# The norm in front of the router, by rows: tokens centred and scaled while they stand as rows, then transposed back

## What is computed

```python
def _layernorm(x, axis=-1, eps=1e-05):
    m = jnp.mean(x, axis=axis, keepdims=True)
    v = jnp.var(x, axis=axis, keepdims=True)
    return (x - m) / jnp.sqrt(v + eps)
...
    x = x + _L0_xattn_ref(_layernorm(x, axis=-1), ctx_1024, ctx_1024, ...)
    x = x + _L0_ffn_ref(_layernorm(x, axis=-1), ...)
    x = x + _L1_xattn_ref(_layernorm(x, axis=-1), ctx_1024, ctx_1024, ...)
    x = x + _L1_ffn_ref(_layernorm(x, axis=-1), ...)
```

## Time and profile before

| | us |
|---|---|
| median of 3 runs | 335.76 (335.49 to 336.69) |
| profiled execution | 337.2 |
| its span | 335.0 |
| TensorE busy | 315.0 (94%) |
| VectorE busy | 262.3 (78%) |
| ScalarE busy | 201.6 (60%) |
| GpSimd busy | 45.8 (14%) |

### The profile page before, as it was taken

The page is one execution under the profiler, slowest core; times in us unless marked ns, Lnnn a source line. Parts: engine busy times, 40 slices in busy tenths (PEclk is TensorE's granted clock), DMA queues, the critical chain, the costliest instruction groups (busy, mean ns, idle before and its releaser), DMA issues.

```text
span 335.0 us, 4438 instructions
## 1 busy us (share of the span) xinstructions
PE 315.0 (94%) x1498; PEld 224.1 (67%) x1506; DVE 262.3 (78%) x543; ACT 201.6 (60%) x325; POOL 45.8 (14%) x55
## 2 busy tenths in 40 slices
PE   7999899899999899969879999999999999998995
PEld 7655698556556667656657777777767777766763
DVE  2542674769578997979987989989987996999693
ACT  3514206464687856688878758758367546635733
POOL 0030012121111701164171121000001000000000
PEclk9899999999999999999979999999999999999999
DMA  7999960000000000180440651001001000000001
GB/s 261 427 422 317 297 257 1 0 3 0 0 0 2 1 2 0 63 190 1 132 120 1 179 104 33 0 2 32 0 0 34 0 0 31 3 0 31 2 0 63
DMA packets 13173, 25.21 MB, mean 75 GB/s; under 512 B 608, under 2 KB 9056, under 8 KB 11872
## 3 DMA queue, kind: packets, MB, share of 16 engines
q1 hardware_dynamic: 11712, 20.75, 17.5%
q0 software_dynamic: 1440, 4.19, 6.8%
HBM read 16.55 MB, written 1.05 MB: 53 GB/s over the span
## 4 chain that ended last, share of the span: by engine, by line
PE 80%; DVE 8%; ACT 6%; issue 3%; DMA 2%; POOL 0%; SPq 0%; DVEq 0%; ACTq 0%; POOLq 0%
PE ps L1389 76%; DMA ctxT<-in_ctxT 2%; PE ps L1495 1%; PE ps L1612 1%; ACT ring L560 1%; ACT L610 1%; ACT L575 1%; ACT L560 1%; DVE hm_even L1070 1%; PE ps L1516 1%; ACT hid L612 1%; ACT hB L552 1%; DVE ctxT L1281 1%; DVE kv L1278 1%; DVE ctxT L1280 1%
## 5 line engine op out<-in xcount | busy, mean ns | idle before, releaser
L1389 PE MATMUL ps<-hm_even,ew_hi 128*128 128x512 f32 (+1 forms) x152 | 49.6, 420 | 1.9 <-ACT xi L538 1.2
L1389 PE MATMUL ps<-hm_odd,ew_hi 128*128 128x512 f32 (+1 forms) x148 | 47.6, 422 | 0.0
L1389 PEld LDWEIGHTS ps<-hm_even,ew_hi 128*128 128x128 f32 (+1 forms) x152 | 26.3, 188 | 8.4 <-issue 2.4
L1389 PEld LDWEIGHTS ps<-hm_odd,ew_hi 128*128 128x128 f32 (+1 forms) x148 | 25.7, 189 | 5.5 <-issue 0.5
L612 ACT ACTIVATE hid<-ps,pB 128x512 f32<-128x512 f32 x32 | 21.8, 687 | 11.6 <-PE ps L1389 10.9
L477 POOL TENSOR_TENSOR zz<-zz,mhalf 128x4 f32<-128x4 f32 x12 | 14.8, 1237 | 91.2 <-DVE zz L943 91.2
L1389 PE MATMUL ps<-hm_even,ew_lo 128*128 128x512 f32 (+1 forms) x72 | 25.2, 392 | 0.0
L1389 PE MATMUL ps<-x_hi,w1x_hi 128*128 128x512 f32 x40 | 19.1, 478 | 5.8 <-ACT hid L612 3.7
L1389 PE MATMUL ps<-hm_odd,ew_lo 128*128 128x512 f32 (+1 forms) x64 | 22.3, 394 | 0.0
L1051 DVE SCALAR_TENSOR_TENSOR ring<-ring,pB,hid 128x1024 f32<-128x1024 bf16 x16 | 20.5, 1281 | 0.6
L1389 PE MATMUL ps<-zz,pB 128*128 128x512 f32 (+3 forms) x52 | 19.4, 502 | 0.5 <-DVE zz L1324 0.5
(11 more groups left out here) (325 smaller groups left out, 769.0 us busy)
## 6 DMA issues: line engine op xcount, KB each, us to landing
ring<-in_fc1b SPq DMA_DIRECT2D x4, 1024.0 KB, 17.3
ring<-in_fc2a SPq DMA_DIRECT2D x4, 1024.0 KB, 12.4
hm_odd<-hm_odd SPq DMA_DIRECT2D x4, 512.0 KB, 3.1
packC<-in_packC SPq DMA_DIRECT2D x1, 1152.0 KB, 9.1
pB<-in_packB SPq DMA_DIRECT2D x1, 1077.0 KB, 9.9
ctxT<-in_ctxT SPq DMA_DIRECT2D x2, 512.0 KB, 6.4
a<-in_fc1a SPq DMA_DIRECT2D x1, 1024.0 KB, 8.9
xtok<-in_xtok SPq DMA_DIRECT2D x1, 1024.0 KB, 12.8
```

The costliest lines, as they stand in the source:

```text
L1389: return pe.matmul(out, lhsT, rhs, start=start, stop=stop)
```

## The change

For the norm in front of the router, mean and factor are applied where the token is a row: `ln_rows` subtracts the mean and multiplies by the factor straight out of the token bank, four VectorE instructions per chunk, into `xi`. `state_back` transposes those four pieces back on TensorE, ScalarE's `state_evac` copies them to `xi`. `center`, the spread of this norm and its multiplication are gone; those of the feed-forward norm stay. Who waited for `zn` now waits for `cx`; the token bank is held until the rows are read. In the first pass of the experts ScalarE's evacuations of chunks 2 and 3 move behind some hidden tiles.

```diff
+        def back_bank(c):
+
+            return bank[5] if c == NCH - 1 else bank[6]
...
+            def ln_rows(c):
+
+                n = LN["rt", c]
+                dve.wait_ge(sem("lrs"), n + 1)
+                for j in range(BPC):
+                    row = slice(j * D, (j + 1) * D)
+                    dve.tensor_scalar(xi[:, ck(c)][:, row], tok_bank(n)[:, row], lmv[:, n % 2, j, 0:1],
+                                      lrs[:, n, j:j + 1], ALU.subtract, ALU.mult).then_inc(sem("rows"), 1)
...
+            def state_evac(c):
 
                 act.wait_ge(sem("cx_ps"), c + 1)
-                act.activation(xi[:, ck(c)], center_bank(c)[:, :], ACT.Copy).then_inc(sem("cx"), 1)
+                act.activation(xi[:, ck(c)], back_bank(c)[:, :], ACT.Copy).then_inc(sem("cx"), 1)
...
                 if t == 3:
                     state_split(0)
                     route(0, 1)
+                if q:
+                    ln_rows(t - 2)
                 if a:
                     att_norm(t - 1)
-                if q:
-                    ln_scale("rt", t - 2)
                 ffn_add(t)
...
             att_pt(3)
-            ln_scale("rt", 2)
+            ln_rows(2)
             kept(0, 2)
...
                     lower(s, 1)
-                    ln_scale("rt", 3)
+                    ln_rows(3)
                     lower(s, 0)
...
-                if n >= 2:
+                if n - 2 in NORMED and n < 3 * NCH - 1:
+                    pe.wait_ge(sem("rows"), BPC * (NORMED[n - 2] + 1))
+                elif n >= 2:
                     pe.wait_ge(sem("lst"), BPC * (n - 1))
...
+            def state_back(c):
+
+                pe.wait_ge(sem("rows"), BPC * (c + 1))
+                if c == 0:
+                    pe.wait_ge(sem("zn"), NCH)
+                elif c < NCH - 1:
+                    pe.wait_ge(sem("cx"), c)
+                else:
                     pe.wait_ge(sem("squash"), 2)
                 for j in range(BPC):
...
+                    row = slice(j * 128, (j + 1) * 128)
+                    last = pe.transpose(back_bank(c)[:, row], xi[:, ck(c)][:, row], ident)
+                last.then_inc(sem("cx_ps"), 1)
...
-                if q:
-                    center(t - 2)
                 ffn_down(t, (0, 1))
                 if q:
-                    ln_spread("rt", t - 2)
+                    state_back(t - 2)
                 ffn_down(t, (2,))
...
             ln_tok("rt", 2, "x3")
-            center(2)
             hidden(0, (2, HT))
...
                     pe.wait_ge(sem("lg"), 2)
-                    pe.wait_ge(sem("cx"), 3)
+                    pe.wait_ge(sem("x3"), 3)
...
                         probs_t(3)
-                        ln_spread("rt", 2)
+                        state_back(2)
...
                     def hidden_0():
-                        center(3)
                         hidden(1, (0,))
 
                     def hidden_2():
                         hidden(1, (2,))
-                        ln_spread("rt", 3)
+                        state_back(3)
```

More of the change, by code:

```diff
@@ L391, in build @@
             LN["rt", c] = len(LN)
-        def spread_at(which, c):
-            return c if which == "ffn" else NCH + c
+        NORMED = {n: c for (which, c), n in LN.items() if which == "rt"}
         @block.sync
@@ L700, in _ @@
             expand_evac(1, 7, 6)
-            hidden_gelus(1, (1,))
-            center_evac(3)
-            hidden_gelus(1, (0, 2, 3))
+            hidden_gelus(1, (1, 0, 2))
+            state_evac(3)
+            hidden_gelus(1, (3,))
             r1_gelu(3)
@@ L944, in ln_stats, with ln_scale @@
                     .then_inc(sem("lve"), 1)
[L946 to L956, removed]
+            def ln_scale(c):
+                dve.wait_ge(sem("spread_ps"), c + 1)
+                if c >= 2:
+                    dve.wait_ge(sem("fh_ps"), FT * (c - 1))
+                dve.tensor_tensor(zT[:, c % 2, :], xT[:, ck(c)], bank[6][:, :], ALU.mult).then_inc(sem("zn"), 1)
+            def ln_rows(c):
[5 more added lines that the diff above has]
+                                      lrs[:, n, j:j + 1], ALU.subtract, ALU.mult).then_inc(sem("rows"), 1)
             def att_scores(c):
@@ L1503, in busy, with ln_spread @@
                     mm(out, ew2_hi[:, 0:D], ew2_hi[:, 0:CH])
-            def ln_spread(which, c):
-                n, at = LN[which, c], spread_at(which, c)
-                if at == 0:
+            def ln_spread(c):
+                n = LN["ffn", c]
+                if c == 0:
                     pe.wait_ge(sem("w1"), 2)
                 else:
-                    pe.wait_ge(sem("zn"), at)
+                    pe.wait_ge(sem("zn"), c)
                 pe.wait_ge(sem("lrs"), n + 1)
-                if at == 2 * NCH - 1:
+                for j in range(BPC):
+                    last = pe.transpose(bank[6][:, j * 128:(j + 1) * 128],
+                                        lrs[:, n, j:j + 1].to_broadcast([128, 128]), ident)
+                last.then_inc(sem("spread_ps"), 1)
+            def state_back(c):
+                pe.wait_ge(sem("rows"), BPC * (c + 1))
+                if c == 0:
+                    pe.wait_ge(sem("zn"), NCH)
+                elif c < NCH - 1:
+                    pe.wait_ge(sem("cx"), c)
+                else:
                     pe.wait_ge(sem("squash"), 2)
                 for j in range(BPC):
-                    last = pe.transpose(spread_bank(which, c)[:, j * 128:(j + 1) * 128],
-                                        lrs[:, n, j:j + 1].to_broadcast([128, 128]), ident)
-                last.then_inc(sem("spread_ps"), 1)
[L1520 to L1525, removed]
+                    row = slice(j * 128, (j + 1) * 128)
+                    last = pe.transpose(back_bank(c)[:, row], xi[:, ck(c)][:, row], ident)
+                last.then_inc(sem("cx_ps"), 1)
             def ffn_up(c, tiles):
-                pe.wait_ge(sem("zn"), spread_at("ffn", c) + 1)
+                pe.wait_ge(sem("zn"), c + 1)
                 for f in tiles:
```

35 lines of the change are left out of this document (16 added, 19 removed).

## The result

The changed kernel takes 347.43 us (median of 4 executions, 346.14 to 350.0), the kernel before 335.62 beside it: a ratio of 1.0358, 95% interval 1.0326 to 1.0391. It is slower by 11.8 us, in the direction that was forecast; 343.2 was given, and 347.43 lies 0.4 us above the range. The profiled execution is the one of 350.0 us, so its times are 2.6 us above the median.

The account below looks back on a forecast made before the run. TensorE was taken as the bound, other engines counting where it waits for them. Terms of -0.6, +1.45, +2.35 and +1.8 make +5.0; with +2.4 for the clock, 335.76 + 7.4 = 343.2 us, range 339.0 to 347.0.

Parts of the forecast that it names:

- TensorE waits for the rows, in order: Before the transposes back, TensorE waits about 0.3, 2.3, 3.5 or more, and 2.7 us at chunks 0 to 3.
- Crediting nothing for the 1.18 us: TensorE's wait for ScalarE's evacuation of chunk 2 goes, but waits for VectorE stand close behind: no gain counted.
- I take 1.0: Four VectorE row instructions per chunk cost 1.0 us, between bounds of 0.88 and 1.12.
- Chunk 0 gains 0.6: At t = 2 the rows fit VectorE's idle time and the addition starts earlier: -0.6 us.
- The sum without clock, +5.0: Delay over all four chunks, before any clock fall: -0.6, +1.45, +2.35 and +1.8 make +5.0 us.
- "+2.4" for the clock: Slow clock behind the three long waits: 1.4 us for the longest, 0.5 each for the other two.
- the row of 2.04 us: TensorE's wait before 171.06 us in the kernel before, after which the granted clock stood at 0.50.
- The rival with a fall behind each wait: A clock fall of 1.4 us behind each of three waits: 9.4 us in all, 345.2 us; chance 0.15.
- Nothing comes back later: TensorE's later waits of 0.85, 1.69 and 2.04 us move along with the delay, so nothing is given back.
- VectorE does not make it good, TensorE is the bound: At chunk 2 the +3.2 us stays, since VectorE needs that chunk's logits from TensorE, which carries 80% of the chain.

Follow-up runs that it names:

- back_later: Changed kernel with the transposes back of chunks 1, 2 and 3 later in TensorE's order, ScalarE's copies moved along, VectorE's order kept: 338.14 us, ratio 1.0066.
- only_0: Kernel before with the new path for chunk 0 alone: 335.54 us, ratio 0.9984.
- only_3: Kernel before with the new path for chunk 3 alone: 340.53 us, ratio 1.0123.
- one_factor: Changed kernel with rows that only subtract the mean, the factor left out (one operand by partition): 345.41 us, ratio 1.0298.
- filled: Changed kernel with 8, 17 and 11 useless TensorE products ahead of the waits for rows of chunks 1, 2 and 3: 342.12 us, ratio 1.0177.
- the best version: Kernel before with new path for chunks 0, 1, 3; chunk 1's transposes back later, chunk 3's transposes to tokens, statistics and rows early: 334.89 us, ratio 0.9969.
- the first combination: Changed kernel, transposes back of chunks 1 and 2 later on TensorE, chunk 3's transposes to tokens, statistics and rows earlier: 338.47 us, ratio 1.006.
- combined_c: Changed kernel, transposes back of chunks 1 and 2 later, chunk 3's rows earlier, 3 and 5 useless products in two TensorE gaps: 337.27 us, ratio 1.002.
- rows_first: Changed kernel with only VectorE's order altered, rows of chunks 1, 2 and 3 ahead of splits and routing: 342.65 us, ratio 1.0184.
- only_1: Kernel before with the new path for chunk 1 alone: 340.08 us, ratio 1.0112.

## Why the prediction was right, and where it was off

- **TensorE waits for the rows, in order.** Right, at each chunk: 0.53, 2.45, 4.40 and 2.90 us, where 0.3, 2.3, 3.5 or more, and 2.7 were given. Crediting nothing for the 1.18 us that ended on ScalarE was right too: 0.23 and 0.90 us took its place. `back_later` shows that it is TensorE's order, and `only_0` to `only_3` that the chunks add up.
- **"I take 1.0"** for four rows was too little: 1.36 us. Both bounds came from instructions with at most one operand by partition. `one_factor` shows that with one the upper bound was exact (4.5 us for 16, so 1.12 for four), and that the second adds the rest: its four waits are 9.3 us and not 10.3, 0.25 each. A bound of 1.12 that leaves out an operand was no bound.
- **Chunk 0 gains 0.6.** The sign was right, the size is 0.4 in the trace: TensorE's wait for that addition fell from 0.54 to 0.16 us, because the rows kept TensorE 0.53 us and the last down product came later than reckoned. In the time of `only_0` the 0.5 us cannot be told from nothing.
- **The sum without clock, +5.0.** 5.9 us in `filled` (1.0155 to 1.0199 is 5.2 to 6.7). With rows of 1.36 us the prediction's own sum is 6.1, 0.36 more in each of three stages, so the dearer rows account for the rest.
- **"+2.4" for the clock** is the step that failed. It gave 1.4 us to the longest wait and 0.5 to each of the two nearer to the row of 2.04 us, since slow time may fall into the wait. The runs showed 1.5, 2.6 and 1.6 us, 5.7 in place of 2.4. In the profiled execution all three waits were followed by a fall, not one or two, and little of the slow time lay in them: the granted clock drops at 102.5 to 103.0 us (0.75), 123.0 to 123.5 (0.73) and 147.0 to 147.5 (0.63), while the waits end at 102.99, 124.34 and 146.50. At chunk 2 the slow stretch was also longer than the eight products on which 1.4 rested: 0.50 throughout 124 to 128 us and 0.74 behind it. So the mechanism was right and its size was not. With both sizes put right the prediction's sum is 335.76 + 6.1 + 5.7 = 347.6. The rival with a fall behind each wait had the mechanism, but with 1.4 it was short too; and its sum is wrong, since 5.0 + 3 x 1.4 is 9.2 and gives 345.0, not 345.2.
- **Nothing comes back later.** Right: the later waits kept their size.
- **VectorE does not make it good, TensorE is the bound.** Right for the change as made. It did not carry over to the cure: once TensorE no longer waits, VectorE's unbroken chain sets the first expert pass, and the three centring products saved in the best version brought 1.0 us, not 0.86 each. My expectation of 334.5 for the first combination made that error. That of 336.2 for the third made another, that full clock always shortens the path: in `combined_c` it did not, because TensorE was not the last there.

What stays open in part: why the profiled execution of the change took 2.6 us more than the median. Its trace has a fourth slow stretch, where the kernel before has its own at 171 us:

```profile
184.00:188.00 4.00, 4.00 (x11) 2.63 (x12) 3.90 (x5) 2.29 (x5) 3.73 (x4) 0.58 0.60 115
```

Its mean granted clock is 0.975, that of the three others 0.980, 0.980 and 0.984. By clock and length, an estimate, the others spent some 3.6 to 6.4 us less at half clock. At 3.4 us of half clock this stretch can account for 1.7 us at most; the rest stays open.

## What to carry to other kernels

Where a result is moved from an engine with room to another, look first at the order of the engine that waits: at the place in TensorE's order where the new operand is due, and at what could run ahead of it. Here the same instructions cost 11.8 us, or 2.2 with the transposes a few products later. Price a new instruction by a row with as many operands of the same kind, and count for each long wait of TensorE the slow stretch behind it, in us of the work that stands there; here it was 1.5 to 2.6 us each.

## What the runs showed of the hardware

The second operand by partition costs VectorE 60 ns in a 128 x 128 instruction from PSUM (342 to 402), and the first one 59 ns in a 128 x 512 instruction from SBUF (692 to 751); a second operation without one costs nothing there (692 and 692).

The granted clock does not follow the length of one wait alone. In `back_later` waits of 0.23, 0.90 and 1.27 us close together were followed by 0.50, and in the same run 1.50 us alone (before 139.33) left the clock at 1.00. In `rows_first` 1.64 us (before 103.54) left it there too, and 1.92 us (before 139.75) did not. The Trainium skill ("TensorE: Matmul & The Clock Gate", section "Why this matters for your kernels") asks for no long idle gaps between bursts; the changed kernel agrees at its three waits. That all three are long in the sense of the page was the prediction's reading, not the page's words. Nor was such a wait always followed by a fall: in the profiled execution of `only_1` the same wait was 2.46 us, and its stretches behind it:

```profile
100.00:104.00 4.00, 1.54 (x11) 0.97 (x11) 3.04 (x14) 2.56 (x11) 0.00 (x0) 1.00 0.02 4
104.00:108.00 4.00, 4.00 (x31) 3.27 (x29) 2.56 (x8) 3.06 (x4) 0.00 (x0) 1.00 0.00 0
```

That execution took 338.92 us, the others of the kernel 339.67 to 340.54; the mean granted clock is 0.995 in it and in the one of 339.67, and 0.99 in the other two, as one more slow stretch would give. The fall that the kernel before has at 171 us is not in every execution either: of 13 executions of that kernel beside these runs, seven have a mean granted clock of 0.999 or 1.000 and six of 0.994 or 0.995. In 168 to 184 us the profiled execution of `only_0` stands at full clock:

```profile
168.00:184.00 16.00, 13.82 (x67) 9.57 (x66) 14.37 (x17) 13.75 (x20) 7.06 (x9) 1.00 0.20 42
```

That of `only_3` does not:

```profile
168.00:184.00 16.00, 13.05 (x52) 8.94 (x52) 11.73 (x16) 12.57 (x20) 6.95 (x9) 0.89 0.41 96
```

The same wait can thus be followed by a slow stretch in one execution and by none in another; a forecast of a fall is a chance, not a rule.
